# Second matrix product two chunks behind the first instead of three, in the feed-forward stage of a fused attention and feed-forward layer

## The reference, cut to what matters

```python
xn = layernorm(x)                                   # x: 16 x 2048 x 1024
Q, K, V = xn @ Wq, xn @ Wk, xn @ Wv                 # 1024 -> 128
attn = softmax(causal(Q @ K.T * 128**-0.5)) @ V
hidden = xn @ W1 + b1                               # 1024 -> 4096
imag = w_imag * sin(theta + hidden * 0.1)
phase = cos(theta) * w_real + sin(theta) * w_imag
act = relu(hidden + phase * imag * 0.1)
out = x + attn @ Wo + act @ W2 + b2                 # 4096 -> 1024
```

## Time and profile before

| | us |
|---|---|
| median of nine runs | 1248.51 |
| the profiled execution, its own time | 1248.26 |
| its span on the slowest core (core 0) | 1246.5 |
| spans of the eight cores | 1237.8 to 1246.5 |
| TensorE busy with matmuls | 1075.8 (86%) |
| ScalarE busy | 595.5 (48%) |
| VectorE busy | 453.1 (36%) |

### The profile page before, as it was taken

The page is one execution under the profiler, slowest core; times in us unless marked ns, Lnnn a source line. Parts: engine busy times, 40 slices in busy tenths (PEclk is TensorE's granted clock), DMA queues, the critical chain, the costliest instruction groups (busy, mean ns, idle before and its releaser), DMA issues.

```text
span 1246.5 us, 23746 instructions; the slowest of 8 cores (1237.8 to 1246.5 us)
## 1 busy us (share of the span) xinstructions
PE 1075.8 (86%) x7810; PEld 737.8 (59%) x7936; DVE 453.1 (36%) x1007; ACT 595.5 (48%) x1285; POOL 37.0 (3%) x48
## 2 busy tenths in 40 slices
PE   0756675779898989898989898989898989999998
PEld 0744574456565656565656565656565656566665
DVE  2726653623232333233333233333333333333332
ACT  2865584535354545354535454545444444444443
POOL 1220021000000000000000000000000000000000
PEclk9978785889999999999999999999999999999999
DMA  7869778920202020202020202020202020202010
GB/s 156 246 116 199 169 221 141 168 82 2 85 1 86 1 85 1 85 1 85 1 85 1 85 1 85 2 85 2 85 1 85 1 85 1 85 1 86 7 46 35
DMA packets 47416, 87.13 MB, mean 70 GB/s; under 512 B 7106, under 2 KB 23490, under 8 KB 46274
## 3 DMA queue, kind: packets, MB, share of 16 engines
q1 hardware_dynamic: 36226, 59.39, 15.0%
q0 software_dynamic: 11072, 26.22, 11.6%
HBM read 78.25 MB, written 25.17 MB: 83 GB/s over the span
## 4 chain that ended last, share of the span: by engine, by line
PE 74%; DVEq 2%; issue 2%; DVE 2%
PE psW L821 37%; PE psOut L847 35%; PE psOut L837 2%; DVEq L767 2%; DVE probs L769 1%; DVE u_sb L746 0%; DVE out_sb L769 0%; DVEq L774 0%; DVEq L745 0%; DVEq L766 0%; DVEq L743 0%
## 5 line engine op out<-in xcount | busy, mean ns | idle before, releaser
L821 PE MATMUL psW<-xn_r,W_sb 128*128 128x256 bf16 x4096 | 541.9, 276 | 56.2 <-DVE u_sb L746 50.5
L821 PEld LDWEIGHTS psW<-xn_r,W_sb 128*128 128x128 bf16 x4096 | 404.5, 99 | 220.2 <-issue 65.2
L847 PE MATMUL psOut<-W_sb,rb_sb 128*128 128x512 bf16 x1936 | 512.8, 381 | 5.9
L746 DVE SCALAR_TENSOR_TENSOR u_sb<-ss_sb,Rp_sb,psW 128x256 f32<-128x256 bf16 x512 | 244.5, 480 | 590.5 <-ACT ss_sb L786 576.1
L786 ACT ACTIVATE ss_sb<-psW,phb_sb 128x256 bf16<-128x256 f32 x512 | 241.9, 473 | 445.9 <-PE psW L821 445.7
L794 ACT ACTIVATE rb_sb<-u_sb,b_sb 128x256 bf16<-128x256 f32 x511 | 254.5, 498 | 83.4 <-DVE u_sb L746 81.2
L847 PEld LDWEIGHTS psOut<-W_sb,rb_sb 128*128 128x128 bf16 x2048 | 202.1, 99 | 142.0 <-issue 9.7
L622 DVE CAST pT_big<-psT 128x512 bf16<-128x512 f32 (+2 forms) x80 | 48.9, 612 | 39.4 <-PE psT L546 35.1
L440 PE MATMUL psTx<-diag_li,probs 128*128 128x128 bf16 x176 | 15.9, 243 | 41.0 <-DVE diag_li L328 38.5
L769 DVE TENSOR_TENSOR out_sb<-psOut,out_sb 128x512 f32<-128x512 f32 x32 | 20.6, 686 | 77.5 <-PE psOut L847 77.5
L546 PE MATMUL psT<-diag_li,xn_rg 128*128 128x128 bf16 x272 | 30.0, 252 | 18.7 <-DVE pT_big L622 16.4
(11 more groups left out here) (91 smaller groups left out, 428.9 us busy)
## 6 DMA issues: line engine op xcount, KB each, us to landing
x_sb<-x SPq DMA_DIRECT2D x52, 512.0 KB, 5.4
W_sb<-w POOLq DMA_DIRECT2D x8, 2048.0 KB, 45.7
xn_scr<-xn_rg POOLq DMA_DIRECT2D x32, 256.0 KB, 4.2
xn_r<-xn_scr SPq DMA_DIRECT2D x16, 512.0 KB, 7.2
out<-out_sb SPq DMA_DIRECT2D x32, 256.0 KB, 2.1
out<-probs SPq DMA_DIRECT2D x32, 256.0 KB, 4.8
xn_r<-x SPq DMA_DIRECT2D x12, 512.0 KB, 6.5
Q_fm<-b2rep SPq DMA_DIRECT2D x1, 512.0 KB, 3.5
```

Source lines behind the costliest of these rows:

```text
L746: su2.inc(v.scalar_tensor_tensor(u2_sb[ci % 2][:], ss_sb[ci % 2][:], Rp_sb[:, c:c + 1], psW1[slot][:], ALU.mult, ALU.add))
L821: ins = t.matmul(psW1[slot][:], W1_sb[:, k * DFF + c * 128: k * DFF + (c + 1) * 128], xn_r3[g % 2][:, k * R3:(k + 1) * R3], start=(k == 0) ...
L847: ins = t.matmul(psOut[tt][:, h * 512:(h + 1) * 512], rb_sb[cw % 3][:, tt * 128:(tt + 1) * 128], W2_sb[:, cc * D + h * 512: cc * D + (h + ...
```

## The change

The loop on TensorE runs two turns past the last chunk instead of three, and down of a turn is that of the chunk two turns back, not three. Nothing is added or removed: the counts of all instructions, their operands, the buffers and what each instruction waits for stay. The order on the other four engines is the same row for row.

```diff
-                    for ci in range(NCHG + 3):
+                    for ci in range(NCHG + 2):
...
-                        cw = ci - 3
+                        cw = ci - 2
```

## The result

The changed kernel takes 1222.9 us, the median of ten runs, beside 1248.64 us for the kernel before; the ratio is 0.979 (95% interval 0.978 to 0.980). Forecast were 1223 us. All ratios here, and the times of the last two experiments, leave out executions in which the cores of one die ran disturbed, since these show a lower clock and longer times whatever the kernel (1405.6 us in the longest of the changed kernel's, with a granted clock of 0.80 on the mean of one die and 0.95 on the other), and the rows of the last experiment are from a core of the undisturbed die. The profiled execution took 1223.52 us; its slowest core is core 4, with a span of 1221.6 us.

What follows compares the result with a forecast made beforehand. The prediction took the 15 group boundaries, 5.12 us lost at each, as what the change can reach. From 1248.26 us, 38.4 us gained less 12.7 us clock and 0.6 us end gave 1223 us; range 1209 to 1235 us.

Steps and rivals of the forecast that it cites:

- What bounds the kernel: At 15 group boundaries up waits for mix queued behind additions: 5.12 us lost each, 3.53 stop and 1.59 clock.
- The stop after the change: At each boundary down(32) waits for relu(32), with 0.25 us release: 2.56 us lost as stop, against 3.53 us.
- The clock: Behind boundary stops the clock falls to half speed at 8 of 15 boundaries, costing 1.59 us each.
- The rival from the Trainium skill: At the boundaries, gaps of 0.9 us at most cause no fall of the clock: 1210.5 us, chance 0.25.
- Rounds within a group: Inside groups the shorter lag still covers relu, 0.35 us to spare, thinner at chunk 17: no cost, rounds 1.737 us.
- The end of the stage: Behind up(511), the last down is due before relu(511) is released: 0.6 us lost, once.
- The sum: Over the whole kernel: 38.4 us gained, 12.7 us given back by the clock, 0.6 us lost; net 25.1 us.

Runs made afterwards that it cites:

- the last two experiments: Matmuls whose result nothing reads put into the boundary stops: six in the changed kernel, 1211.9 and 1213.2 us; 14 in the kernel before, 1225 to 1228 us.
- the last experiment: The kernel before with 14 added matmuls, read by nothing, behind the last down of each of the first 15 groups: 1225 to 1228 us, ratio 0.983.
- a kernel in which the boundaries cost 0.16 us: Against the kernel before: mix of two chunks ahead of the additions, downs of chunks 30 and 31 two behind, up(36) ahead of Wo matmuls; 1175.41 us.

## Why the prediction was right, point by point

- **What bounds the kernel.** Right: undoing the change at the boundary alone gives back the whole time, and a kernel in which the boundaries cost 0.16 us runs 73 us faster than before, close to 15 x (5.12 - 0.16) = 74.4 us.
- **The stop after the change.** Right in its mechanism, too large by 0.12 us: 2.44 us measured for 2.56. The term that was mis-sized is the release of down by ScalarE. The prediction took 0.25 us from the earlier trace rows, and bounded it by 0.14 us from below. relu ended at 503.97 + 0.51 = 504.48 and down started at 504.62: 0.14 us, the lower bound. The kernel with lag one shows the same 0.14 us in its rounds. In the source the matmul of the earlier trace rows stands behind two waits, for `sqke` and then for `stxe`, and down behind one; whether that makes its 0.25 us was not tried.
- **The clock.** Right in size and about right in number: eight falls of 15 forecast, seven on the profiled core, each worth 60.55 - 58.88 = 1.67 us against 1.59. The count was a choice between rows that pointed both ways; the runs show where a mixture lies. The stop of 2.44 us lies between one that a fall follows nearly always (3.53 us, at 119 of the 120 boundaries of the eight cores before) and one that none follows (1.61 us, in the two kernels with mix ahead of the additions). Why every second boundary has a fall and the ones between have none is not shown: the 15 stops of the profiled core are alike within 0.01 us.
- **The rival from the Trainium skill**, page "TensorE: Matmul & The Clock Gate", section "Why this matters for your kernels", that long idle gaps between bursts cause the falls: as the only cause, the measurement differs. At the third boundary, where the clock fell, the fourth Wo matmul and down(96) stand like this:

```profile
443.03 0.38 PE L837 MATMUL psOut<-Wo_sb,o_fm 128*128 128x512 bf16 x1 [0.22 <-DVE probs L769]
...
444.07 1.82 PE L847 MATMUL psOut<-W_sb,rb_sb 128*128 128x512 bf16 x4 [0.67 <-ACT rb_sb L794]
```

  The longest gap left is 444.07 less the end of the fourth Wo matmul, 443.03 + 0.22 (a quarter of the 0.87 us of four), so 0.82 us, and the clock still fell at seven boundaries. Several short gaps in one stretch did what one long gap does.
- **Rounds within a group.** Right: no wait there, also not behind the additions of chunk 16. With the release of 0.14 us the spare of 0.35 us is 0.46 us; in the trace after, relu ends 0.61 us ahead of its down in nearly every round (0.47 us of it spare), and 0.36 us ahead in the round of chunk 17.
- **The end of the stage.** The size was near, the place was missed: it is down(510) that waits for relu, and down(511) is late mostly because down(510) was. In the profile after:

```profile
1211.83 1.04 PE L821 MATMUL psW<-xn_r,W_sb 128*128 128x256 bf16 x8
...
1212.70 1.03 PE L847 MATMUL psOut<-W_sb,rb_sb 128*128 128x512 bf16 x4
...
1213.97 1.94 PE L847 MATMUL psOut<-W_sb,rb_sb 128*128 128x512 bf16 x8 [0.25 <-ACT rb_sb L794]
```

  down(510) would be due at 1212.70 + 0.87 = 1213.57 and starts 0.40 us later. No up stands between the last downs any more, so a lag of two turns is less time there. The price is 0.4 to 0.5 us instead of 0.6.
- **The sum.** With the measured sizes: 15 x (5.12 - 2.44) = 40.2 us, less 7 x 1.67 = 11.7 us, less 0.4 us, is 28.1 us, for 25.1 us forecast. Of the 3.0 us between them the stop makes 1.8, the count and size of the falls 1.0 and the end 0.2. The fifth stage itself, from its first up to the end of the span, is 27.7 us shorter (987.9 us before, 960.2 us after), but the two profiled executions differ by only 1248.26 - 1223.52 = 24.7 us. The rest lies ahead of the stage: its first up starts at 258.65 us in the chain of before (core 0) and at 261.42 us after (core 4); first the row of before, then that of after,

```profile
258.65 5.92 PE psW L821 x32
```

```profile
261.42 5.28 PE psW L821 x24
```

  2.8 us later, in stages that the change does not touch. That the forecast hit within 0.1 us is therefore luck in the last 3 us: a stop that was too long in the sum, and one fall too many, met a slowest core that began its last stage later.

## What to carry to other kernels

When a pipeline stops at the seams between groups, look for the work of the next group that is queued behind the last work of the old one on a helping engine; putting that one instruction ahead gained twice what the shorter lag gained. A shorter lag is free only as long as the chain behind it is covered: here two turns left 0.46 us, and one turn cost 600 us. Price a stop of TensorE with the half-speed stretch behind it, and ask of a shortened stop whether that stretch goes as well, since here it was a third of the cost.

## What the runs showed of the hardware

Falls of the clock came in a regular pattern, at every second boundary from the third to the last on the profiled core, though all its stops are alike (2.43 to 2.44 us). A stretch in which TensorE is used thinly but evenly can keep the clock: the rounds of the kernel with lag one, 1.27 us of each 3.01 us unused, ran at 1.00. A stop cut into five gaps of at most 0.82 us, 2.44 us unused in 3.31 us, was followed by 0.50 at seven of 15 boundaries, and cost 1.67 us each time. Matmuls that compute nothing useful, put into a stop, made both kernels faster, by 0.8% (ratio 0.9715 against 0.979) and by 1.7% (ratio 0.983).
